# A transformer decoder block on one core: rough scores moved to the unit's end, one SP gather and one key rope moved, and the front and tail reordered

## The reference

```python
x = x + attn(layernorm(x))      # 128 heads: 4 content dims from a 64-wide latent, 64 rotary-slot dims
x = x + xattn(layernorm(x), ctx, ctx, positions)   # 32 query heads, 8 key heads of 16, with rotary
x = x + ffn(layernorm(x))       # dense 512x512 plus top-2 of 8 low-rank experts of rank 16
```

## Time and profile before

| | |
|---|---|
| median of 3 runs | 826.92 us (826.72 to 828.41) |
| the profiled execution | 826.78 us |
| its span in the profile | 824.5 us |
| TensorE, DVE, ACT, POOL busy | 96%, 76%, 71%, 72% of the span |
| DMA moved | 75.80 MB, 92 GB/s on average |

### The profile page before, as it was taken

The page is one execution under the profiler, slowest core; times in us unless marked ns, Lnnn a source line. Parts: engine busy times, 40 slices in busy tenths (PEclk is TensorE's granted clock), DMA queues, the critical chain, the costliest instruction groups (busy, mean ns, idle before and its releaser), DMA issues.

```text
span 824.5 us, 17894 instructions
## 1 busy us (share of the span) xinstructions
PE 793.0 (96%) x5641; PEld 391.9 (48%) x5641; DVE 628.6 (76%) x1190; ACT 582.7 (71%) x1072; POOL 590.9 (72%) x535
## 2 busy tenths in 40 slices
PE   5999999999999999999999999999999899999987
PEld 3464444444444444444444444444444444555444
DVE  6766676676677788776788876778878888888766
ACT  8757777777777777777777777778765655666551
POOL 7967999999988888887888887878655634222111
PEclk9999999999999999999999999999999999999999
DMA  9344355533434333343333344352321000000001
GB/s 344 124 172 142 93 142 161 162 98 89 104 107 120 90 79 93 89 128 100 100 81 97 83 119 107 92 158 63 88 61 48 27 2 2 14 14 13 18 15 39
DMA packets 52176, 75.80 MB, mean 92 GB/s; under 512 B 10256, under 2 KB 34096, under 8 KB 51616
## 3 DMA queue, kind: packets, MB, share of 16 engines
q1 hardware_dynamic: 52128, 75.23, 32.8%
HBM read 38.69 MB, written 19.40 MB: 70 GB/s over the span
## 4 chain that ended last, share of the span: by engine, by line
PE 87%; DVE 4%; ACT 3%; issue 2%; SPq 2%; DMA 1%; POOL 0%; DVEq 0%; ACTq 0%
PE PS L1567 40%; PE PS L1639 7%; PE PS L1606 7%; PE PS L1640 7%; PE PS L1501 6%; PE PS L1654 5%; PE PS L1740 2%; PE PS L1832 2%; PE PS L1679 1%; PE PS L1798 1%; PE PS L1616 1%; PE PS L1688 1%; PE PS L1839 1%; PE PS L1817 1%; PE PS L1849 1%
## 5 line engine op out<-in xcount | busy, mean ns | idle before, releaser
L1567 PE MATMUL PS<-XTh,W 128*128 128x512 f16 x1024 | 346.0, 379 | 0.0
L656 POOL TENSOR_TENSOR Pl<-PR,Ph 128x512 f16<-128x512 f32 x254 | 285.8, 1156 | 28.4 <-ACT Ph L938 28.4
L931 ACT ACTIVATE PR<-PS 128x512 f32<-128x512 f32 x256 | 152.8, 597 | 131.7 <-PE PS L1640 124.9
L1125 DVE TENSOR_REDUCE mneg<-PS 128x4 f16<-128x512 f32 x256 | 171.6, 685 | 35.3 <-PE PS L1606 33.4
L1567 PE MATMUL PS<-XTl,W 128*128 128x512 f16 x512 | 193.6, 378 | 0.0
L1113 DVE SCALAR_TENSOR_TENSOR QS<-PS,QC 64x512 f16<-64x512 f32 x256 | 175.5, 685 | 20.8 <-ACT QC L848 16.7
L848 ACT ACTIVATE QC<-PS 64x512 f16<-64x512 f32 x256 | 150.7, 589 | 9.2 <-PE PS L1567 4.3
L1567 PEld LDWEIGHTS PS<-XTh,W 128*128 128x128 f16 x1024 | 96.6, 97 | 118.8 <-issue 25.9
L938 ACT ACTIVATE Ph<-PR 128x512 f16<-128x512 f32 x256 | 139.3, 617 | 0.0
L1606 PEld LDWEIGHTS PS<-KC,QC 112*128 112x128 f16 x1024 | 78.4, 97 | 63.5 <-issue 2.7
L1606 PE MATMUL PS<-KC,QC 112*128 112x128 f16 x1024 | 99.4, 219 | 0.9 <-ACT QC L848 0.8
(11 more groups left out here) (236 smaller groups left out, 1034.1 us busy)
## 6 DMA issues: line engine op xcount, KB each, us to landing
Wraw<-in_wqr SPq DMA_DIRECT2D x32, 512.0 KB, 4.8
QS<-QC SPq DMA_DIRECT2D x64, 256.0 KB, 3.2
head_outputs<-OS SPq DMA_DIRECT2D x256, 40.0 KB
q_content_parts<-stg SPq DMA_DIRECT2D x12, 256.0 KB, 2.9
k_content_parts<-stg SPq DMA_DIRECT2D x12, 256.0 KB, 3.1
QC<-q_content_parts SPq DMA_DIRECT2D x116, 24.0 KB
KC<-k_content_parts SPq DMA_DIRECT2D x29, 96.0 KB
xs<-in_x SPq DMA_DIRECT2D x8, 256.0 KB, 4.8
```

Source lines behind the costliest of these rows:

```text
L656: nc.gpsimd.tensor_tensor(Pl[:, 4 * j.s + b], PR[:, b], Ph[:, 4 * j.s + b], ALU.subtract).then_inc(s_pl, 1)
L931: nc.scalar.activation(PR[:, b, :], PS[:, bB[b % 2], :], ACT.Exp, scale=ATT_SCALE).then_inc(s_e, 1)
L1125: nc.vector.tensor_reduce(mneg[:, j.p, j.s, :, b], PS[:, bA[b % 2], :].rearrange("p (j k) -> p j k", j=GH), AX.X, ALU.max, negate=True).th ...
L1567: last = mm(PS[:, bQ[c], :], wt[:, j.w, k, c * P:(c + 1) * P], xt[:, k, sl], start=(i == 0), stop=(i == 3 * KT - 1))
```

## The change

Eleven places, by engine:

- SP: the last `quarter` gather of sum 2 and the first `late_contents` move from before half 58 into `late_half(58)`, behind `maxima` and `q_again`.
- POOL and ACT: xn of all odd batches is made by POOL, of the even ones by ACT; ACT's order of x_high, weight split and xn is rewritten. ACT casts the rest of the context after the rotary key's high part.
- TensorE's front: the rotary key projection stands before the first four contents and writes both halves to bank 1; the second projection waits for its readers.
- DVE: `k_rope(1)` runs in unit 5 instead of 1; unit 7 does the query's rope before `x_outputs`.
- TensorE's units: `x_rough(u + 2)` stands last in the unit; in unit 8 `norm_turn(2, 0)` follows `x_scores`; batch 5's first base product stands in unit 31.
- Tail: base banks are 2, 3 and 7 for batches 5, 6 and 7; batch 7's third base product follows its `low_turn`.

```diff
@@ -363,8 +363,7 @@
         def base_bank(v):
-
-            return bF[1] if v < B - 2 else 2 + v % 2
+            return {B - 3: 2, B - 2: 3}.get(v, bF[1])
@@ -372,7 +371,7 @@
             return [(CS[:, w], 2 + t, RD * w, t) for t in range(2) for w in range(2)] + \
-                [(KS, 2 + t, RD * t, t) for t in range(2)]
+                [(KS, bQ[1], RD * t, t) for t in range(2)]
@@ -495,6 +494,9 @@
                 q_again(job(h - 1))
+                if h == LATE:
+                    late_contents(job(LATE))
+                    quarter(KT - 2, GH - 1)
                 if h + 1 < NH:
@@ -546,8 +548,8 @@
                     spelled(half, 8 * T + 9 + j, 8 * T + 9 + j)
-                    quarter(T, j)
-            late_contents(job(LATE))
+                    if (T, j) != (KT - 2, GH - 1):
+                        quarter(T, j)
             for h in range(LATE, NH):
@@ -609,11 +611,10 @@
                 nc.gpsimd.tensor_tensor(mv[:, 0, 2 * i:2 * i + 2, 0], mv[:, 0, 2 * i:2 * i + 2, 0], part, ALU.mult).then_inc(n_sd[0], 1)
-                if i >= 2:
-                    b = 2 * i + 1
-                    pool.wait_ge(n_sd[0], i + 1)
-                    nc.gpsimd.tensor_scalar(xn[:, b, :], xs[:, b, :], rstd[:, 0, b:b + 1], mv[:, 0, b, 0:1],
-                                            ALU.mult, ALU.add).then_inc(s_pp, 1)
+                b = 2 * i + 1
+                pool.wait_ge(n_sd[0], i + 1)
+                nc.gpsimd.tensor_scalar(xn[:, b, :], xs[:, b, :], rstd[:, 0, b:b + 1], mv[:, 0, b, 0:1],
+                                        ALU.mult, ALU.add).then_inc(s_pp, 1)
@@ -874,16 +875,16 @@
-            for b in range(4):
-                normed(b)
+            normed(0)
+            normed(2)
             x_high(0)
+            normed(4)
             x_high(1)
...
             nc.scalar.activation(wd_h[:], wd_raw[:], ACT.Copy, scale=WS).then_inc(s_wdh, 1)
-            normed(4)
             x_high(2)
+            normed(6)
             x_high(3)
-            normed(6)
             act.wait_ge(s_up, 16)
@@ -898,10 +899,10 @@
                 up_high(i)
+            latent_high(4)
+            latent_high(5)
             for k in range(1, KT):
                 ctx_high(k)
-            latent_high(4)
-            latent_high(5)
             for c in range(4):
@@ -1255,7 +1256,7 @@
                     dve.wait_ge(s_kvr, 1)
-                    dve.wait_ge(s_xqa, 2)
+                    dve.wait_ge(s_xqa, 3)
                 krt = rt[:].rearrange("p a (b n) -> p a b n", b=B // 2)
@@ -1416,7 +1417,7 @@
                     x2(b - 1, bF[1])
-                if 0 <= u - 1 < NU:
+                if 0 <= u - 1 < NU and u != 7:
                     x_outputs(u - 1)
@@ -1425,7 +1426,7 @@
                             dve.wait_ge(s_xqa, v)
-                        if v >= 2:
+                        if v >= 3:
                             dve.wait_ge(s_kvr, 2)
@@ -1435,6 +1436,8 @@
                         nc.vector.tensor_tensor(qr[:], rt[:, 0], rt[:, 1], ALU.add).then_inc(s_xqa, 1)
+                if u == 7:
+                    x_outputs(u - 1)
                 if r == 1:
@@ -1457,7 +1460,7 @@
                     x1(3)
-                if u == 1:
+                if u == 5:
                     k_rope(1)
@@ -1504,10 +1507,7 @@
             for b in range(B):
-                if b in (5, 7):
-                    pe.wait_ge(s_pp, b // 2 - 1)
-                else:
-                    pe.wait_ge(n_xn[0], b + 1 if b < 5 else 6)
+                pe.wait_ge(s_pp if b % 2 else n_xn[0], b // 2 + 1)
                 if b >= 6:
@@ -1536,7 +1536,7 @@
                 else:
-                    pe.wait_ge(s_pp, 4)
+                    pe.wait_ge(s_pp, B // 2 + 2)
                     bank_read("u", i)
@@ -1569,19 +1569,21 @@
-            pe.wait_ge(s_pp, 3)
-            for i in range(4):
-                up_content(i)
-
             for k in range(KT):
...
                     for t in range(2):
-                        last = mm(PS[RD * t:RD * (t + 1), 2 + t, :], wt[:, k, 2 * LAT:], xt[:, k, t * HALF:(t + 1) * HALF],
+                        last = mm(PS[RD * t:RD * (t + 1), bQ[1], :], wt[:, k, 2 * LAT:], xt[:, k, t * HALF:(t + 1) * HALF],
                                   start=(k == 0 and n == 0), stop=(k == KT - 1 and n == 2))
...
+            pe.wait_ge(s_pp, B // 2 + 1)
+            for i in range(4):
+                up_content(i)
+
             for c in range(4):
+                if c == 1:
+                    pe.wait_ge(s_cl, 6)
                 for k in range(KT):
@@ -1888,6 +1890,8 @@
                     turn(u + 2)
+                if u == NU - 1:
+                    base(B - 3, 0)
                 if 0 <= u - 2 < NU:
@@ -1901,7 +1905,8 @@
                         lora(v)
-                    norm_turn(2, b - 2, bF[0])
+                    if u != 8:
+                        norm_turn(2, b - 2, bF[0])
                 if r == 2:
@@ -1931,10 +1936,6 @@
                     keep_clock(3)
-                if u == -2:
-                    pe.wait_ge(s_x1, B // 2)
-                if 0 <= u + 2 < NU:
-                    x_rough(u + 2)
                 if r == 2:
@@ -1943,22 +1944,26 @@
                     x_scores(u)
+                if u == 8:
+                    norm_turn(2, 0, bF[0])
                 if 0 <= u - 1 < NU:
                     x_weigh(u - 1)
+                if u == -2:
+                    pe.wait_ge(s_x1, B // 2)
+                if 0 <= u + 2 < NU:
+                    x_rough(u + 2)
...
             x_weigh(NU - 1)
-            take(bF[1], s_x3, B - 2)
-            base(B - 3, 0)
+            base(B - 3, 1)
             x_back(NU - 1)
...
             project_outputs(B - 1, bP7)
-            base(B - 3, 1)
             base(B - 3, 2)
@@ -1969,10 +1974,11 @@
             lora(B - 2)
-            for n in range(3):
-                last = base(B - 1, n)
-            last.then_inc(s_o2, 1)
+            take(bF[1], s_x3, B)
+            base(B - 1, 0)
+            base(B - 1, 1)
             low_turn(B - 1)
+            base(B - 1, 2).then_inc(s_o2, 1)
             lora(B - 1)
```

## The result

The kernel after takes **830.91 us** (median of 6 runs, 830.39 to 831.26), the kernel before 827.56 in the runs beside it: a ratio of 1.0040 (95% interval 1.0027 to 1.0053). It is slower by 3.35 us. The prediction was 830.3. The profiled execution is the longest of the six: 831.26 us, its span 829.6, 5.0 more than the span of before.

What follows compares the result with a forecast made beforehand. TensorE was taken as the bound, busy for 96% of the span; 826.78 - 0.9 + 2.1 + 1.7 - 0.2 + 0.4 + 0.45 gave 830.3 us. Range 823.5 to 832.3, the forecast's own 828.5 to 832.3.

Steps and rivals of the forecast that it cites:

- The sum: Whole kernel: all terms together +3.55 us on the profiled 826.78, so 830.3 us; chance 0.52.
- Rivals 1 to 3: 1: clock holds, 828.6, chance 0.15; 2: gather early or absorbed, 827.1, 0.16; 3: outputs_turn no longer waits, some 820, 0.17.
- rival 3: Cross attention: DVE's x_outputs comes early enough for outputs_turn; up to -9, some 820, halfway 823; chance 0.17.
- Late gather: Halves 58 and 59: gather lands 4.0 us after U's issue, DVE stands, TensorE stalls 2.7 and 0.45 us; +2.1 us.
- the row QS<-QC: Gather's landing time: sized by the trace's 256 KB transfer on the same queue, 3.2 us, not by the skill's rule.
- The clock: Behind half 58's new stall: 3.4 us at half speed, +1.7 us, bounds 0 and 1.7; no fall near 685.
- Front: First transposes and projections: xn shared with POOL and reordering end waits; -0.9 us, bounds -1.6 and 0.
- Units -2 to 9: Early cross attention: key rope leaves unit 1, new waits come in units 1 to 8; -0.2 us, bounds -2 and +2.
- Units 10 to 24: Steady cross attention: rough scores at the unit's end cost +0.4 us in all, for units 13, 17 and 21.
- The step on outputs_turn: Steady cycle: TensorE waits 0.70 us at outputs_turn for DVE's x_outputs, in place of 0.56 us at the rough scores.
- +0.14 us a cycle: Steady cycle: outputs_turn starts at 732.6 and 0.33 us of rough scores is still owed, against 732.79 before.
- Units 25 to the end: Last units and tail: low_turn waits, the 0.37 us wait for lowT is covered; +0.45 us, bounds -1 and +1.5.

Runs made afterwards that it cites:

- b_sp: Kernel before with SP's part of the change alone (last gather of sum 2 and late contents 58 behind maxima 56): 830.82 us, ratio 1.0036.
- a_gather_mid: Kernel after with the gather ahead of late contents 58 instead of behind them, still behind maxima 56 and q_again: 826.90 us, ratio 0.9992.
- a_filler: Kernel after with twelve unused 512-column matmuls put where TensorE stalls, ahead of the turn of the maxima: 829.56 us, ratio 1.0022.
- a_rough_mid: Kernel after with the rough scores between the turns and this unit's scores: 828.62 us, ratio 1.0019.
- a_gather_early: Kernel after with the gather back ahead of half 58, late contents still behind the maxima: 825.87 us, ratio 0.9980.
- b_front: Kernel before with the front alone (odd batches' xn by POOL, rotary key projection first in one bank, ACT's cast order): 826.47 us, ratio 0.9991.
- b_krope: Kernel before with the key rope in unit 5 and unit 7's query rope ahead of the outputs, rough scores unmoved: 825.60 us, ratio 0.9983.
- c_steady: c_best with the rough scores at the unit's end in units 10 to 24 only: 820.53 us, ratio 0.9920.
- b_cross: Kernel before with all of cross attention's change (b_krope plus rough scores at the unit's end and unit 8's norm_turn): 828.73 us, ratio 1.0022.
- c_best: Kernel after with the gather back ahead of half 58, rough scores and unit 8's norm_turn back in their old places: 822.70 us, ratio 0.9944.
- c_turn_late: c_steady with the outputs' turn behind the turn of the maxima and the scores in units 13, 17 and 21: 821.45 us, ratio 0.9932.

## Why the prediction was right, and where it was not

**The sum** is right: +3.55 predicted, +3.35 between the medians, and 830.91 within the forecast's own range. But it was worked out against the profiled execution, and between the profiled executions the loss is 4.5 us, 5.0 within the span. In those terms it was 1.5 short, and the terms below are compared in them. Rivals 1 to 3 did not come true: the clock did not hold, the gather was not early, outputs_turn did wait. Two slips in the recorded sums changed nothing: 2.7 + 0.45 less 1.23 is 1.9 and not 2.1, and rival 3's terms add up to -10.1, while its "up to -9" would be 817.8 and not 820.

**Late gather: right by its own steps.** Predicted were a landing 4.0 us after U's issue, DVE standing for it, a stall of 2.7 and one of 0.45. Measured in the kernel after: 3.94, 4.37 and 3.10. The second stall is 0.47 in b_sp, a_gather_mid, a_filler and a_rough_mid; in the kernel after the half clock had begun before it and hid it. DVE's last row maximum ends at 559.85, where 560.8 less the front's 0.9 had it; the stall is 0.4 larger because TensorE arrives 1.3 us sooner (556.80 for 558.12) and not 0.9. With b_sp's second stall the stall part is +2.3 (3.10 + 0.47 less 1.23; +2.1 predicted). The saved 1.23 us is no part of the gather's bargain: a_gather_early saves 0.89 of it too, with its gather in the old place. By the Trainium skill (DMA: Bandwidth & Descriptors, "Anatomy of one DMA") the landing would have been at some 3.1 us and the half at +1.2. That section gives its figure for DMAs issued by GpSimd, which the prediction did not say; this gather is issued by SP. The measured 3.94 decides for the row QS<-QC.

**The clock: right in kind, short in size.** It fell behind the new stall in after, b_sp and a_rough_mid, and did not fall near 685 in the kernel after. b_sp's 3.4 us at half clock cost 1.79 us (2.26 between the turns less 0.47), near the 1.7 predicted; the 6.8 us of the kernel after cost 2.35. The prediction counted one fall of 3.4 us; every execution of the kernel after has some 8 us or more. That the stall in half 58 causes the fall behind it is shown: of the profiled executions the three with a stall of 3.1 us there lost the clock, the ten with 0.86 us or none kept it, and so did a_filler, with matmuls put into the stall. The Trainium skill (TensorE: Matmul & The Clock Gate, "HAM oscillation") names only longer idle gaps as the danger; these traces do not agree, with falls behind waits of 1.76 us (before) and 1.53 us (a_filler).

**Front: right in sum, wrong in its working.** -0.9 predicted, -0.89 at the first projection of the context (41.13 us before) in the profiles of after and b_front. By half 57 it is -1.21 in the kernel after and still -0.89 in b_front. But I overlooked that DVE's low part of x becomes late (1.17 us of new waits), and what balances it is the clock's earlier rise, which I had only as a bound.

**Units -2 to 9: failed by 1.3 us** (-0.2 predicted, +1.1 measured). The 1.35 in unit 1 was right (1.46). Unit 2 waits 1.41 and not 0.75, unit 4 0.79 and not 0.35, unit 5 1.27 and not 0.95. Unit 8 has 1.18 and 0.52 for 0.75 and 0.6. One wait is missing from the list:

```profile
682.13 1.02 PE L1504 MATMUL PS<-Wxh,Ah 128*128 128x512 f16 x4 [1.32 <-DVE Al L1304]
```

DVE's second key rope, moved into unit 5, takes no less time there (1.72 us for its sine products, L1267, for 1.77 in unit 1) and holds the engine until 681.4, and the low part that unit 7's query needs comes behind it. b_krope has this wait too (1.00 us) and still wins 1.67 us over these units; the rough scores' move then takes 2.8 back. The waits that I had too small or not at all add up to some 3 us, more than the miss; what starts earlier in these units, as x_back does below, was not taken apart.

**Units 10 to 24: wrong in sign** (+0.4 predicted, -1.4 measured). The step on outputs_turn was right: its wait is 0.81 us a cycle for 0.70 predicted, and the stall did change its name. The step that failed is its conclusion, "+0.14 us a cycle": I counted the rough scores as work owed and did not ask what starts earlier when they go last. x_back does, by 0.2 us a unit, and the cycle from unit 18 on is 0.58 shorter. The gain in units 10 to 24 is shown by c_steady, x_back's part in it by the starts and by a_rough_mid, which put the wait back.

**Units 25 to the end: under-sized** (+0.45 predicted, +1.9 in this profile). About 1.6 of it is the half clock at 788: b_cross, with the same order and full clock there, loses 0.67 from unit 25 to 29 where the kernel after loses 2.31. So the waits were right, and the term that failed is again the clock's, which had no second fall. low_turn is late as predicted, and the wait for lowT is gone.

So three things failed: the waits of units -2 to 9 (1.3 us too good), the step "+0.14 us a cycle" (1.8 too bad) and the count of the clock's falls (0.65 too good at half 58, 1.6 at 788). The first two have opposite signs and nearly cancelled; what was left of the third was hidden by 0.6 us won outside the span, which the prediction did not have, and by profiled executions that lay 0.8 below (before) and 0.35 above (after) their medians. By the medians, cross attention and tail together cost +0.39 against +0.65 predicted. A right total was thus partly luck; that the late gather and the clock behind it cost more than the whole change, 3.5 us against 3.35, was not.

## What to carry to other kernels

When a step is moved behind others in a DMA queue, look up who waits for it and what stands ahead of it: 2.3 us of other issues put ahead of a gather became 2.24 us of stall (kernel after against a_gather_mid), and half clock came on top. When work is moved to a stage's end, step through both what becomes late and what starts earlier, on every engine, and use starts and not only listed waits: 0.1 to 0.3 us a unit was hidden under the tail of a matmul. And judge a move by stage: the one that cost 3 us over all units pays 1.6 us in the steady ones, and c_steady, which keeps it only there and leaves the gather alone, beats the kernel before by 6.5 us and the kernel after by some 10.

## What the hardware showed that was not expected

The granted clock fell in places that no single wait explains. Of the ten profiled executions with a wait of 1.3 us or more in cross attention, nine had a stretch at half clock there or in the tail, at 657, 685, 781, 788, 801 or 803 us, and kernels with the same waits had it in different places; b_sp, with the same 1.76 us wait as before, kept the full clock there. The four kernels whose longest wait there is about 1.1 us (b_krope, c_best, c_steady, c_turn_late) had none. The mean granted clock of all executions says the same, less sharply: it is 0.999 or more in all 16 executions of the three c kernels, in 7 of 10 of b_krope, in 20 of 83 of the kernel before, 3 of 10 of b_front, 1 of 10 of a_gather_early and in none of the 65 other ones. One and the same kernel thus has the fall in some executions and not in others. They are also four of the five lowest medians.

The last gather of sum 2, U and SU, took 3.94 us from U's issue to DVE's start in the kernel after, 3.95 in b_sp, 4.01 in a_rough_mid, 4.79 in a_gather_mid, 5.07 in c_turn_late, 5.11 in a_gather_early and 5.24 in a_filler. The forecast's 4.0 is at the lower end, and what makes it longer was not tried; on this record a wait that stands in the path should be sized with 5.

The same eight matmuls of the rough scores hold TensorE for 0.33 us in their old place, where a turn follows them, and for 0.33 us behind x_weigh, but for 0.23 us between the turn of the maxima and the scores, which read the same tile KQ. Which of the neighbours makes the difference was not tried.
